# Four samples at a time, with all four layers folded into nine taps, in place of two samples and seven taps

## The reference

```python
TYPES = ('same', 'upsample', 'same', 'downsample')
def _layer(x, style, w, b, mw, mb, typ):
    s = style @ mw.T + mb
    weight = SCALE * w * s[:, None, :, None]
    demod = lax.rsqrt(jnp.sum(weight * weight, axis=(2, 3)) + EPS)
    weight = weight * demod[:, :, None, None]
    ...
    if typ == 'same':
        out = jax.vmap(_conv_same)(x, weight) + b[None, :, None]
    elif typ == 'upsample':
        out = jax.vmap(_conv_up)(x, weight.transpose(0, 2, 1, 3)) + b[None, :, None]
        out = _blur(out, 2.0 * blur_k, (1, 1))
    elif typ == 'downsample':
        xb = _blur(x, blur_k, (2, 2))
        out = jax.vmap(_conv_down)(xb, weight) + b[None, :, None]
...
out = x
for i, typ in enumerate(TYPES):
    out = _layer(out, style, weights[i], biases[i], mod_w[i], mod_b[i], typ)
x = x + out
```

## Time and profile before

| | us |
|---|---|
| median of 3 runs | 167.99 |
| lowest and highest run | 167.83, 169.42 |
| span of the profiled execution | 166.5 |
| PE busy in it | 158.8 |
| VectorE, GpSimd, ScalarE busy | 131.8, 94.4, 56.4 |

### The profile page before, as it was taken

How to read it: one execution, slowest core, us unless ns; L and a number is a source line. 1 busy time by engine, 2 the same in 40 slices (tenths; PEclk the granted TensorE clock), 3 DMA queues, 4 the chain that set the end, 5 groups by cost and what they waited for, 6 DMA issues and landing times. The chain is left out here.

```text
span 166.5 us, 8946 instructions
## 1 busy us (share of the span) xinstructions
PE 158.8 (95%) x3975; PEld 146.1 (88%) x3975; DVE 131.8 (79%) x229; ACT 56.4 (34%) x127; POOL 94.4 (57%) x155
## 2 busy tenths in 40 slices
PE   7999999999999999999999999999999999999970
PEld 5687888959789789999899999999999999999960
DVE  7859877788868869778696969696979797969993
ACT  3245561323142332334251514243434334231120
POOL 7209908596493977456373829191919192837530
PEclk9959999999999999999999999999999999999998
DMA  4982000120302204335343445353634242030314
GB/s 119 274 212 14 2 4 4 55 79 4 125 8 65 68 4 126 130 130 190 105 183 118 182 133 186 129 193 111 213 110 145 88 143 101 7 126 4 132 74 180
DMA packets 13990, 17.81 MB, mean 107 GB/s; under 512 B 5216, under 2 KB 5760, under 8 KB 13952
## 3 DMA queue, kind: packets, MB, share of 16 engines
q1 hardware_dynamic: 13888, 17.22, 31.1%
...
HBM read 8.85 MB, written 8.39 MB: 104 GB/s over the span
## 5 line engine op out<-in xcount | busy, mean ns | idle before, releaser
L190 POOL TENSOR_TENSOR Hw<-Hw 128x192 f32<-128x192 f32 x15 | 9.0, 598 | 50.8 <-DVE Hw L885 50.8
L546 PE MATMUL p_m<-uu,Hw 64*64 64x128 f32 x992 | 31.6, 269 | 0.0
L546 PEld LDWEIGHTS p_m<-uu,Hw 64*64 64x64 f32 x992 | 29.4, 132 | 0.1
L466 PE MATMUL p_lo<-xin,w0s 64*64 64x259 f32 x384 | 27.7, 406 | 0.1
L309 POOL COPY Hw<-Hw 64x896 f32<-64x896 f32 x15 | 25.8, 1722 | 1.0
L466 PE MATMUL p_le<-xin,w0s 64*64 64x260 f32 x384 | 26.3, 389 | 0.0
L511 PE MATMUL p_le<-R_sb,F_st 64*64 64x128 f32 (+2 forms) x768 | 25.8, 266 | 0.3 <-issue 0.3
L536 PE MATMUL p_m<-u,Hw 64*64 64x256 f32 x384 | 25.4, 375 | 0.0
L896 DVE TENSOR_TENSOR uu<-u 128x516 f32<-128x516 f32 x32 | 24.3, 796 | 1.4
L911 DVE TENSOR_TENSOR e_sb<-p_lo,s_sb 128x512 f32<-128x512 f32 x16 | 11.1, 696 | 16.8 <-PE p_lo L546 16.6
L511 PEld LDWEIGHTS p_le<-R_sb,F_st 64*64 64x64 f32 x768 | 23.3, 133 | 1.1 <-issue 0.9
...
## 6 DMA issues: line engine op xcount, KB each, us to landing
xin<-in_x_dram SPq DMA_DIRECT2D x32, 256.0 KB, 3.3
out_dram<-ot SPq DMA_DIRECT2D x32, 256.0 KB, 2.4
...
bn<-in_L_cond_mod_b_dram ACTq DMA_DIRECT2D x1, 1.0 KB
bn<-in_L_cond_biases_dram ACTq DMA_DIRECT2D x1, 1.0 KB
```

Source lines behind the costliest of these rows:

```text
L466: ins = pe.matmul(bank[h * C:(h + 1) * C, s, 0:n], w0s[p % 2][rows, k, :], xin[p % NX][rows, i0:i0 + 2 * n - 1:2], start=(k == 0), stop=(k ...
L546: ins = pe.matmul(bank(h)[s * C:(s + 1) * C], tap(p, h, s, blk), moving(slice(h * C, (h + 1) * C), s, k), start=(k == 0), stop=(k == len(b ...
```

## The change

The kernel is written anew around quads: eight groups of four samples (`QUADS`), two on the rows and two side by side in the free dimension.

- **Nine taps.** Layer 0 is no longer run by itself. After `compose_R` and `compose_H` a third composition, `compose_T`, multiplies the seven taps `H_sb` by layer 0's weights `W0_st`. PE writes eight of the nine blocks to `p_h` and one to `p_k`; ScalarE moves them to `Tw`, scaled by layer 0's style (`evac_T`). The input that is added at the end goes in as an identity: `add_ident` adds the identity, divided by the last demodulation factor, to the middle tap.
- **The products** act on the input itself, on four phases of the output (positions modulo four). For each quad there are 22 products of 256 columns: `product_a2` (3, on every fourth position of `xin`), `product_bc2` (5, on `dx_sb`), `product_a13` (5, on every second element of `d_sb`), `product_bc1` (5) and `product_bc3` (4), both on `dd_sb`. `d_sb` and `dd_sb` are differences and differences of differences, made by VectorE with 2072 and 2064 elements each (`make_d`, `make_dd`); `dx_sb` is made by GpSimd (`make_dx`, 1032 elements). Two PSUM tiles `p_c` take turns: `product_a2` and `product_a13`, then `product_bc3` go to one, `product_bc2` and `product_bc1` to the other, and each waits until what was in it has been read.
- **VectorE adds** the identity and makes the sums of taps (`add_ident`, `sum_blocks`), which GpSimd did for `Hw`; the blocks come out on both halves, and `place_H` is gone. The sums of the next quad stand between `make_s` and `make_e` of this one. `make_s` (2 instructions of 512 elements), `make_e` (4 of 512) and `finish` (2 times 2 of 508) scale by the last demodulation factor and add the parts; `finish` writes every fourth position of the output tile.
- **Around it:** loads and stores are 512 KB each; the ends are four outputs wide; GpSimd's prologue no longer waits for `e2`, and `make_dx(0)` stands ahead of its products.

```diff
+        def add_ident(eng, q):
+            wait(eng, T_ident, q)
+            eng.tensor_tensor(di_sb[:], ident2[:].unsqueeze(1).to_broadcast([P, 2, C]),
+                              pvec[:, W_ID, 2 * q:2 * q + 2].unsqueeze(2).to_broadcast([P, 2, C]), ALU.mult)\
+                .then_inc(di_made, 1)
+            eng.wait_ge(T_evac, 4 * (q + 1))
+            eng.wait_ge(di_made, q + 1)
+            w = Tw[q % NW][:, 4]
+            eng.tensor_tensor(w, w, di_sb[:], ALU.add).then_inc(T_ident, 1)
+        def sum_blocks(eng, q):
+            w = Tw[q % NW]
+            eng.wait_ge(T_ident, q + 1)
+            eng.tensor_tensor(w[:, B_S:B_S + 4], w[:, 8:0:-2], w[:, 7:0:-2], ALU.add).then_inc(T_sums, 1)
+            blk = 2 * C
+            a = w[:]
+            eng.tensor_tensor(w[:, B_U:B_U + 4].rearrange("p (a b) j c -> p a b (j c)", b=2),
+                              view(a, 8 * blk, ((-4 * blk, 2), (-blk, 2), (1, blk))),
+                              view(a, 6 * blk, ((-4 * blk, 2), (-blk, 2), (1, blk))), ALU.add).then_inc(T_sums, 1)
+            eng.wait_ge(T_sums, 3 * q + 1)
+            eng.tensor_tensor(w[:, B_SS:B_SS + 2], w[:, B_S:B_S + 4:2], w[:, B_S + 1:B_S + 4:2], ALU.add).then_inc(T_sums, 1)
...
-            pool.wait_ge(made["e2"], 1)
...
+            make_dx(pool, 0)
...
-            def place_H(p):
-                w = Hw[p % NW]
-                pool.wait_ge(H_sums, 3 * (p + 1))
-                pool.tensor_copy(w[C:P, 1], w[0:C, 0]).then_inc(H_placed, 1)
-                pool.wait_ge(H_placed, 2 * p - 1)
-                pool.tensor_copy(w[0:C, 1], w[C:P, 0]).then_inc(H_placed, 1)
-                pool.wait_ge(H_placed, 2 * p)
...
+            def product_a2(q):
+                bank = p_c[q % 2]
+                pe.wait_ge(T_sums, 3 * (q + 1))
+                pe.wait_ge(x_loaded[q % NX], 32 * (q // NX + 1))
+                wait(pe, y02_made, 2 * q)
+                a = xin[q % NX]
+                part(q, bank, 0, (B_SS, B_SS + 1, 0),
+                     lambda rows, j, n: a[rows, j, 3 + 4 * n:3 + 4 * n + 4 * NQ - 3:4]).then_inc(a2_done, 1)
...
+                for k, first, n in ((2, 0, NH), (1, 1, NH), (0, 2, NH - 1)):
+                    for i in range(2):
+                        for j in range(2):
+                            rows = slice(j * C, (j + 1) * C)
+                            pe.matmul(p_h[i * C:(i + 1) * C, j, first * C:(first + n) * C], W0_st[rows, k, :],
+                                      H_sb[rows, i, 0:n], start=(k == 2), stop=(k == 0), skip_group_check=True)
...
+                def odd(of):
+                    return lambda rows, j, n: d_sb[rows, j, of, 1 + 2 * n:1 + 2 * n + 2 * NQ - 1:2]
+                part(q, bank, 0, (B_U, B_U + 2, 0), odd(0))
+                part(q, bank, NQ, (B_U + 1, B_U + 3), odd(1)).then_inc(a13_done, 1)
...
-            for p in range(PAIRS):
-                if 0 < p < PAIRS - 1:
-                    layer0_odd(p + 1)
-                    layer0_even(p + 1)
-                if p + 2 < PAIRS:
-                    compose_R(p + 2)
-                if p < 4:
-                    pe.wait_ge(made["e_read"], 2 * (p + 1))
-                product_2(p)
-                if p == 0:
+            for q in range(QUADS):
+                product_a2(q)
+                if 0 < q < QUADS - 1:
+                    compose_H(q + 1)
+                if q == 0:
+                    pe.wait_ge(made["e_read"], 2)
                     pe.wait_ge(made["c"], 2)
-                product_1(p)
-                if p + 2 < PAIRS:
-                    compose_H(p + 2)
-                product_1_mid(p)
-                product_3(p)
-                if p < 3:
-                    pe.wait_ge(s_made, p + 1)
-                if p == 0:
+                if q == 1:
+                    edge_z()
+                product_bc2(q)
+                if q + 1 < QUADS:
+                    compose_T(q + 1)
+                product_a13(q)
+                if q == 0:
                     edge_y()
-                if p == 1:
-                    edge_z()
-                if p == 2:
+                product_bc1(q)
+                if q + 2 < QUADS:
+                    compose_R(q + 2, p_k)
+                if q == 1:
                     edge_out()
+                product_bc3(q)
...
+            def make_d(q):
+                dve.wait_ge(padded, NX)
+                dve.wait_ge(x_loaded[q % NX], 32 * (q // NX + 1))
+                wait(dve, a13_done, q)
+                wait(dve, dd_made, q)
+                a = xin[q % NX][:]
+                dve.tensor_tensor(d_sb[:], view(a, 0, ((XW, 2), (2, 2), (2, ND))),
+                                  view(a, 1, ((XW, 2), (0, 2), (2, ND))), ALU.subtract).then_inc(d_made, 1)
...
+            def make_e(q):
+                dve.wait_ge(a13_done, q + 1)
+                wait(dve, y13_made, 2 * q)
+                for i in range(2):
+                    dve.wait_ge(s_made, 2 * q + i + 1)
+                    for w in range(2):
+                        dve.scalar_tensor_tensor(out=e_sb[:, i, w],
+                                                 in0=p_c[q % 2][:, i, w * NQ:(w + 1) * NQ].unsqueeze(1).to_broadcast([P, 2, NQ]),
+                                                 scalar=pcol(W_D3, 2 * q + i), in1=s_sb[:, i],
+                                                 op0=ALU.mult, op1=ALU.add).then_inc(e_made, 1)
...
+            def finish(q, par, bank, done, signal):
+                dve.wait_ge(done, q + 1)
+                wait(dve, stored[q % NO_T], 32 * (q // NO_T))
+                n = NQ - 2
+                for i in range(2):
+                    dve.wait_ge(e_made, 4 * q + 2 * i + par + 1)
+                    o = ot[q % NO_T][:, i]
+                    dve.scalar_tensor_tensor(out=view(o, 4 + par, ((2, 2), (4, n))),
+                                             in0=bank[:, i].rearrange("p (h n) -> p h n", h=2)[:, :, 1:1 + n],
+                                             scalar=pcol(W_D3, 2 * q + i), in1=e_sb[:, i, par, :, 1:1 + n],
+                                             op0=ALU.mult, op1=ALU.add).then_inc(signal, 1)
...
-            for p in range(PAIRS):
-                if p + 1 < PAIRS:
-                    make_diffs(p + 1)
-                if p + 1 < PAIRS:
-                    make_uu(p + 1)
-                add_parts(p)
-                add_mid(p)
-                if p + 2 < PAIRS:
-                    sum_taps(p + 2)
-                finish(p)
-                if p == 0:
-                    edge_y()
-                if p == 1:
-                    edge_z()
-                if p == 2:
+            for h, rows in enumerate(halves):
+                tt(pgj(W_C, h), gj(p_y[rows, 1, 0:B], h), pgj(W_D3, h), ALU.mult)
+            then()
+            for h, rows in enumerate(halves):
+                ts(pvec[rows, W_C], pvec[rows, W_C], bias[rows, 3:4], None, ALU.add, name="c")
+            make_dd(0)
+            for q in range(QUADS):
+                make_s(q)
+                if q + 1 < QUADS:
+                    add_ident(dve, q + 1)
+                    sum_blocks(dve, q + 1)
+                make_e(q)
+                if q == 0:
+                    scale_edge("ye", one_after_the_other, ye[:], V_E1, WY)
+                finish(q, 0, p_c[(q + 1) % 2], bc1_done, y02_made)
+                if q == 1:
                     edge_out()
-                add_x(p)
+                finish(q, 1, p_c[q % 2], bc3_done, y13_made)
+                if q + 1 < QUADS:
+                    make_d(q + 1)
+                    make_dd(q + 1)
```

944 lines of the change are left out of this document (422 added, 522 removed).

## The result

The changed kernel takes **245.83 us** (four runs, 245.4 to 246.91) where the kernel before, on the same chip, took 168.56: a ratio of 1.455, 95% interval 1.445 to 1.465. The forecast was 165.0 with a range up to 171.5. It is slower by nearly half, and most of the loss lies where the prediction had put 3.8 us.

What follows compares the result with a forecast made beforehand. PE was taken to bound the kernel before; in the new one, PE plus a stall gives 16.77 us a quad. Second `product_bc2` at 51.1, five quads to 135.0, end at 163.4, plus 1.5: 165 us, range 157.5 to 171.5.

Steps and rivals of the forecast that it cites:

- the end: After the last quad: VectorE ends at 159.6 us, the last stores take 3.8 more, span 163.4.
- nearest are two stores back to back: Last 1 MB of stores: 3.8 us taken, between 2.4 if hidden and 9.6 if nothing overlapped.
- the loads are hidden: Loads, twice as large, go out three quads ahead of `product_a2`, so they were to cost nothing.
- PE's work in a quad: PE's products and compositions sum to 15.52 us a quad, 7.76 a pair against 8.57 before.
- The wait that takes its place: PE waits for `make_e` before `product_bc3`, which starts at 8.99 us; a quad becomes 16.77 us.
- the stall: PE idle ahead of `product_bc3`, from 7.74 to 8.99 us: 1.25 us a quad.
- gains nothing by itself: GpSimd's lost sums and copies were hidden behind PE, so removing them was to gain nothing.
- Rival 3: `product_a2`: reading every fourth element costs PE double, eight times 1.36 us more, 175.9 us; chance 0.12.
- Rival 4: Prologue: GpSimd's work beside VectorE's slows eight more operations, 3.1 us with 0.3 taken, 167.8 us; chance 0.12.
- the half clock: Prologue: PE at 1.2 GHz at 9 to 10 us, 2.4 GHz at 12; `compose_R(0)` done by 14.6.
- Rivals 1 and 2: Middle quads: no stall, PE alone, 157.5 us, chance 0.13; or VectorE's loop becomes the bound, 170.7 us, chance 0.18.
- The tail: From VectorE's end to the span's end: 3.8 us for the last stores, bounds -1.4 to +5.8.

Runs made afterwards that it cites:

- all repairs: Changed kernel with stores of 256 KB, woven results, ScalarE's contiguous copy for `product_a2`, and GpSimd's `dx` off VectorE's chain: 172.51 us, ratio 1.028.
- the early copy: Against the kernel with the four repairs, ScalarE makes the contiguous copy right after evacuating H: 169.97 us with sums on VectorE, 165.30 with sums on GpSimd.
- 5.3 us by the experiment: Against the changed kernel with its stores halved, results woven so that `finish` writes every second position: 182.36 us, ratio 1.079.
- with two stores: Changed kernel with each 512 KB store issued as two of 256 KB, one per sample: 187.66 us, ratio 1.110; 58.2 us come back.
- TensorE's new order: Against the kernel with four repairs, `compose_R` goes ahead of `product_bc1` and `compose_H` between `product_bc1` and `product_bc3`: 167.96 us, ratio 0.997.

## Why the prediction was wrong

**The step that failed** is the end, with its "nearest are two stores back to back". It took the store's landing time from the earlier trace rows, of stores of 256 KB whose two samples lie together in memory, for stores that pair samples b and b + 2. The uncertainty was sought in how many stores overlap (2.4 to 9.6 us); that a store could move on two engines was in no rival. At 53 GB/s all 8.39 MB are late, not the last megabyte: 62 us after VectorE's end where 3.8 were taken, and 58.2 us by the experiment. That the loads are hidden held in effect: they did come late behind the stores, but VectorE ended at 181.34 with slow stores and at 181.19 without.

The other terms can be read once the stores and the strides are mended. The middle column is the changed kernel, the last the one with all repairs, the early copy and the sums on VectorE; a group ends where the next one starts:

| | predicted | changed | repaired |
|---|---|---|---|
| first product | 28.9 | 33.27 | 30.46 |
| first `product_bc2` ends | 32.5 | 38.18 | 33.97 |
| second `product_bc2` ends | 51.1 | 59.39 | 53.18 |
| a quad | 16.77 | 18.74 | 16.60 |
| VectorE's last | 159.6 | 181.34 | 161.44 |
| span | 163.4 | 243.6 | 166.8 |

- **PE's work in a quad:** right but for `product_a2`. 15.52 were predicted; with that product made contiguous and no wait left, the quad with GpSimd's sums takes 15.35.
- **The wait that takes its place:** right, and not by luck. `product_bc3` follows `compose_T` after 8.91 us (8.99); in the changed kernel the identity's addition starts at 4.26 (4.31), and it and the sums take 1.87 (1.87). The prediction's terms add up to 8.91, and its 8.93 is a slip without weight. Putting the sums on GpSimd gains the 1.25 us that were named as the stall. That what GpSimd loses "gains nothing by itself" was too mild: VectorE's sums cost 1.25 us a quad, and the two ratios, 1.011 and 0.979, are some 5 us apart.
- **Rival 3 came true.** 2.70 us for `product_a2`, double, eight times 1.34. The upper end was in the working, yet the value was taken from the nearest stride. The rule that was weighed there, of lines of 16 bytes with two accesses each in the Trainium skill's "SBUF — State Buffer", section "Door 1: The DMA port swizzle (why `[64,N]` ≈ `[32,N]`)", agrees in kind on both sides: every second float32 costs next to nothing (1.77 ns a column against 1.70), every fourth the double (3.52), a size that the page does not give.
- **`finish` has the same stride,** and rival 3 was not carried over to it: 0.66 and 0.75 were counted, 1.29 measured. That cost 0.7 us a quad on PE's path and the longer end; 5.3 us by the experiment.
- **Rival 4 came true in part.** The first product was 4.4 us late; 1.2 of it is the half clock in `compose_R(0)`, which the prediction let end too early, and keeping GpSimd away gained 1.3 to 1.8 us up to the first product. Beside `make_dx(0)` two small VectorE operations took 1.82 us, and 0.37 with GpSimd kept away. The same loss in the loop was not foreseen: it appeared as soon as a copy was added to GpSimd.
- **Rivals 1 and 2:** not borne out. The wait for `e_sb` is there, 1.01 us, and none ahead of `product_bc1`. `make_d` and `make_dd` take 2.31 each where nothing lies beside them, 4.62 against 4.7.
- **The tail** with two stores: 5.4 us where 3.8 were taken, inside the bounds. Around the span lie 1.8 us (245.4 against 243.6), not 1.5.

What stays open is the order of the edge stages. The first two quads hold them; the first takes 0.6 us more than predicted, and neither gains by TensorE's new order. A wait for one is seen there, but no other order was tried.
